# Slot selection by matmul, one small product in float32r and a two-step rounding, in a four-layer gated cross-attention kernel

## The reference

```python
x = x + tanh(g_xattn[n]) * xattn_n(layernorm(x), ctx)      # n = 0..3
x = x + tanh(g_ffn[n])   * ffn_n(layernorm(x))
# xattn_1..3: scores = q_r @ k_r^T (16 heads), softmax over 1500, ctx_c = attn @ kv_rope
# ffn_0, a mixture of 64 experts, 6 of them for each token, at most 64 tokens for each expert:
pos  = cumsum(onehot(expert of each assignment)) - onehot     # place of a token in its expert
keep = pos < 64;  slot = where(keep, pos, 64)
xd = zeros((64, 65, 256)).at[expert, slot].set(x[tok])
yd = relu(xd @ w1^T)**2 @ w2^T
y  = zeros_like(x).at[tok].add(yd[expert, slot] * gate)       # plus a shared expert
# ffn_1, with 8-bit activations and ternary weights:
q(x) = clip(round(x * s), -128, 127) / s,  s = 127 / clip(max|x|, 1e-5)
h = silu(q(x) @ qw_gate^T) * (q(x) @ qw_up^T);  h = rms_norm(h);  out = q(h) @ qw_down^T
```

## Time and profile before

| | |
|---|---|
| median of 3 runs | 2315.12 us (2315.03 to 2316.34) |
| profiled execution, its own time | 2315.12 us |
| its span, first to last instruction | 2313.3 us |
| PE busy | 2175.3 us (94%) |
| DVE, ACT, POOL busy | 1529.8, 1029.6, 1482.9 us |
| mean granted TensorE clock | 0.961 |

### The profile page before, as it was taken

How to read it: one execution, slowest core, us unless ns; L and a number is a source line. 1 busy time by engine, 2 the same in 40 slices (tenths; PEclk the granted TensorE clock), 3 DMA queues, 4 the chain that set the end, 5 groups by cost and what they waited for, 6 DMA issues and landing times.

```text
span 2313.3 us, 31038 instructions
## 1 busy us (share of the span) xinstructions
PE 2175.3 (94%) x11468; PEld 1554.3 (67%) x11468; DVE 1529.8 (66%) x2476; ACT 1029.6 (45%) x1509; POOL 1482.9 (64%) x933
## 2 busy tenths in 40 slices
PE   7788999999999997798999999979998999999988
PEld 5577888766666655565666666668896666666587
DVE  6765662578788755766788888652235788888653
ACT  4452222555555544311454555533434555555443
POOL 0355563288888874366688888824443888888744
PEclk9898999999999998898999999999998999999989
DMA  3114767211111103101111111024531111111022
GB/s 91 48 58 155 239 209 207 70 41 42 59 41 41 47 24 117 39 1 41 41 41 41 57 44 41 8 67 146 145 99 54 41 41 61 40 41 42 7 69 74
DMA packets 60593, 160.16 MB, mean 69 GB/s; under 512 B 9621, under 2 KB 19621, under 8 KB 60060
## 3 DMA queue, kind: packets, MB, share of 16 engines
q1 hardware_dynamic: 60060, 157.86, 22.3%
q10 hardware_dynamic: 384, 0.33, 0.1%
HBM read 143.18 MB, written 14.98 MB: 68 GB/s over the span
## 4 chain that ended last, share of the span: by engine, by line
PE 82%; DVE 6%; POOL 3%; ACT 3%; DMA 2%; issue 2%; SPq 0%; POOLq 0%; ACTq 0%; DVEq 0%
PE psum L893 20%; PE psum L1379 19%; PE psum L1369 10%; PE psum L1350 10%; PE psum L1371 10%; PE psum L1527 2%; PE psum L1396 2%; PE psum L1490 1%; DMA V<-in_ctx 1%; PE psum L1264 1%; POOL CL L1814 1%; PE psum L1550 1%; PE psum L1142 1%; DMA WqrT<-in_a_WrT 1%; DMA bd<-in_blockdiag 1%
## 5 line engine op out<-in xcount | busy, mean ns | idle before, releaser
L1792 ACT ACTIVATE E<-psum 125x896 f32<-125x896 f32 x576 | 528.2, 920 | 576.2 <-PE psum L1371 549.3
L2341 DVE TENSOR_REDUCE mx<-psum 128x1 f32<-128x500 f32 x945 | 611.9, 675 | 165.8 <-PE psum L1350 163.8
L2082 POOL TENSOR_TENSOR SA<-SA,E 125x896 f32<-125x896 f32 x282 | 597.3, 2118 | 22.1
L1379 PE MATMUL psum<-E,V 125*64 125x448 f32 x2304 | 472.0, 544 | 0.0
L1369 PE MATMUL psum<-Q,K 128*125 128x448 f32 x1152 | 331.7, 369 | 2.3 <-ACT E L1792 2.3
L1350 PE MATMUL psum<-K,Q 128*128 128x500 f32 x945 | 329.0, 402 | 2.6 <-ACT Q L1779 2.2
L1371 PE MATMUL psum<-Q,K 128*125 128x448 f32 x1152 | 329.8, 367 | 0.0
L1379 PEld LDWEIGHTS psum<-E,V 125*64 125x64 f32 x2304 | 171.6, 136 | 214.0 <-issue 202.6
L2082 POOL TENSOR_TENSOR SA<-SA,SB 125x896 f32<-125x896 f32 x93 | 194.0, 2086 | 148.7 <-DVE SB L2364 148.7
L1350 PEld LDWEIGHTS psum<-K,Q 128*128 128x128 f32 x945 | 174.4, 188 | 134.2 <-issue 34.6
L1369 PEld LDWEIGHTS psum<-Q,K 128*125 128x125 f32 x1152 | 213.1, 187 | 37.2 <-ACT E L1792 6.9
(11 more groups left out here) (296 smaller groups left out, 3649.0 us busy)
## 6 DMA issues: line engine op xcount, KB each, us to landing
K<-kt_scratch SPq DMA_DIRECT2D x48, 750.0 KB, 5.0
K<-kt_scratch SPq DMA_DIRECT2D x48, 375.0 KB, 6.2
EW<-in_f_w SPq DMA_DIRECT2D x64, 256.0 KB, 4.7
kt_scratch<-kt SPq DMA_DIRECT2D x16, 750.0 KB, 4.7
WS<-in_f_w SPq DMA_DIRECT2D x31, 384.0 KB, 4.8
GB<-gates_scratch SPq DMA_DIRECT2D x36, 224.0 KB, 3.7
slot_of_t<-slots_scratch SPq DMA_DIRECT2D x64, 112.0 KB, 3.3
WoT<-in_a_WoT SPq DMA_DIRECT2D x24, 256.0 KB, 4.2
```

Of the source, the lines that this page charges most:

```text
L1379: i = e.matmul(psum[c * DC:(c + 1) * DC, 4 + b % 2, 0:HT], V[0:LP, b, k * DC:(k + 1) * DC], E[g[n, b, k] % NE][0:LP, half[c]], start=k == ...
L1792: e.activation(E[m % NE][0:LP, :].rearrange("p (c q) -> p c q", c=2), psum[0:LP, pair:pair + 2, 0:HT], ACT.Exp).then_inc(exp_set.sem, 1)
L2082: e.tensor_tensor(SA[b % 2][0:LP, :], a[0:LP, :], x[0:LP, :], ALU.add).then_inc(sum_set.sem, 1)
L2341: e.tensor_reduce(mx[:, b % 2, j * 3 + c:j * 3 + c + 1], psum[:, bank, 0:CW], AX.X, ALU.max).then_inc(small_free.sem, 1)
```

## The change

It has three parts.

1. In the experts of layer 0, `pick` moves from POOL and DMA to PE and ACT. The slot number s (-32 to 32) of each token and expert and its square are transposed together (128 rows: s squared for 64 experts, s for 64 experts) and stay in SBUF as GT, float32r. DVE builds weights for each group in a new task `rows` (L2608 ff., 128 x 512, float32r). For each pair and each half of the tokens, PE multiplies 128 x 128 of these weights with 448 columns of GT, which gives s^2 - 2*s*j for slot j; ACT writes S = relu(1 - j^2 - that) = relu(1 - (s - j)^2), which is 1 on equality and 0 otherwise, into the half of S. The 64 new results of PE take their places in the ring of four PSUM banks; comb waits for S by halves. The scratch in HBM, its write and wait, and the 64 broadcasting DMAs go. The tile slot_of holds two planes, and DVE makes the square (448 elements a partition).
2. In the core attentions, nm and the identity of L1357 become float32r; DVE makes the float32r identity once for each layer, after the memset of nm.
3. In the 8-bit part, `quantise` gets a second DVE instruction, which subtracts the rounding constant and takes the minimum with 127, behind a wait for the first; ACT then only copies.

```diff
-    order += [("st", 1, a) for a in range(4)] + [("pload", q) for q in range(3)]
+    order += [("st", 1, a) for a in range(4)]        # ("rows", 0) now stands behind ("route", 7)
...
-        pick = lambda q: [("pick", q)] + ([("pload", q + 3)] if q + 3 < E0 // 2 else [])
-        steps = [[("ups", g)] + ([("gsl", 0)] if g == 0 else []), pick(q),
+        steps = [[("ups", g)] + ([("gsl", 0)] if g == 0 else []), [("pick", q, 0), ("pick", q, 1)],
                  [("comb", q - 1)] if g > 0 else [], ([("disp", g + 1, 0)] if more else []) + st(0),
-                 [("downs", q), ("downs", q + 1)], pick(q + 1) + st(1), [("comb", q)],
+                 [("downs", q), ("downs", q + 1)], [("pick", q + 1, 0), ("pick", q + 1, 1)] + st(1), [("comb", q)],
                  ([("disp", g + 1, 1)] if more else []) + st(2), [("downs", q + 2), ("downs", q + 3)],
-                 pick(q + 2), [("comb", q + 1)] + st(3),
-                 [("gsl", g + 1)] if more else [], pick(q + 3), [("comb", q + 2)]]
+                 [("pick", q + 2, 0), ("pick", q + 2, 1)] + ([("rows", g + 1)] if more else []), [("comb", q + 1)] + st(3),
+                 [("gsl", g + 1)] if more else [], [("pick", q + 3, 0), ("pick", q + 3, 1)], [("comb", q + 2)]]
...
-        if t[0] in ("disp", "gsl", "ups", "downs"):            # upper_uses
+        if t[0] in ("disp", "gsl", "ups", "downs", "pick"):
...
-                e.matmul(psum[0:DC, bank, 0:P], nm[:, b % 2, :], ident[:, :], start=True, stop=True).then_inc(small_made.sem, 1)
+                e.matmul(psum[0:DC, bank, 0:P], nm[:, b % 2, :], identr[:, :], start=True, stop=True).then_inc(small_made.sem, 1)
...
+            elif kind == "pick":                                # PE
+                q, c = t
+                bank = upper(e, f, kind, q, c)
+                if q == 0:
+                    e.wait_ge(*gt_set.at(f, 1))
+                e.wait_ge(*rows_set.at(q // 4))
+                pair = m["rows"][q // 4 % 2][:, q % 4 * 2:q % 4 * 2 + 2, :].rearrange("p k c -> p (k c)")
+                e.matmul(psum[:, bank, 0:HT], pair, m["GT"][:, half[c]], start=True, stop=True).then_inc(matched.sem, 1)
             elif kind == "comb":
                 q, = t
                 e.wait_ge(*ydl_set.at(q))
-                e.wait_ge(*s_set.at(q))
                 for c in range(2):
+                    e.wait_ge(*s_set.at(q, c))
...
+            elif kind == "pick":                                # ACT
+                q, c = t
+                e.wait_ge(*matched.at(q, c))
+                if q >= 2:
+                    e.wait_ge(*combined.at(q - 2, c))
+                e.activation(m["S"][q % 2][:, half[c]], psum[:, upper_bank[f, (kind, q, c)], 0:HT], ACT.Relu, scale=-1.0,
+                             bias=m["slots"][:, 2 * CAP0 + 16:2 * CAP0 + 17]).then_inc(s_set.sem, 1)
...
-            elif kind == "pick":                                # POOL
-                q, = t
-                e.wait_ge(*pb_in.at(q))
-                if q >= 2:
-                    e.wait_ge(*combined.at(q - 2, 1))
-                e.tensor_scalar(m["S"][q % 2][:, :], m["PB"][q % 3][:, :], m["slots"][:, CAP0:CAP0 + 1], None,
-                                ALU.is_equal).then_inc(s_set.sem, 1)
...
-        e.memset(nm[:, :, :], 0.0).then_inc(*dve_own.up())
+        e.memset(nm[:, :, :].bitcast(F32), 0.0)
+        e.tensor_copy(identr[:, :], ident[:, :]).then_inc(*dve_own.up())
...
-        e.tensor_scalar(x, x, scale, ROUND, ALU.mult, ALU.add).then_inc(signal.sem, 1)
+        e.tensor_scalar(x, x, scale, ROUND, ALU.mult, ALU.add).then_inc(*dve_own.up())
+        e.wait_ge(*dve_own.now())
+        e.tensor_scalar(x, x, ROUND, 127.0, ALU.subtract, ALU.min).then_inc(signal.sem, 1)
...
-                             ACT.Copy, bias=-ROUND).then_inc(xqt_set.sem, 1)
+                             ACT.Copy).then_inc(xqt_set.sem, 1)
```

More of the change, by code:

```diff
@@ L129, in constants @@
     slot = np.tile((np.arange(CAP0) - CAP0 // 2).astype(f), (P, 1))
-    c["slots"] = np.concatenate([slot, slot.T[np.arange(P) % CAP0, 0:1]], 1).astype(f)
+    parts = [slot, np.where(np.arange(P)[:, None] < E0, f(1.0), -2.0 * slot), np.tile(np.arange(8, dtype=f), (P, 1)),
+             (np.arange(P)[:, None] % E0 - 8 * np.arange(NG)[None, :]).astype(f), 1.0 - slot.T[np.arange(P) % CAP0, 0:1] ** 2]
+    c["slots"] = np.concatenate(parts, 1).astype(f)
     return c
@@ L232, in sparse_order @@
     order += [("wload", e) for e in range(4, 12)] + side.pop(0)
-    order += [("route", 6)] + [("st", 0, a) for a in range(4)] + [("route", 7), ("disp", 0, 0), ("route", 8), ("disp", 0, 1)]
-    order += [("st", 1, a) for a in range(4)] + [("pload", q) for q in range(3)]
+    order += [("route", 6)] + [("st", 0, a) for a in range(4)] + [("route", 7), ("rows", 0), ("disp", 0, 0), ("route", 8), ("disp", 0, 1)]
+    order += [("st", 1, a) for a in range(4)]
     for g in range(NG):
@@ L389, in upper_uses @@
             out.append(("pos",))
-        elif t[0] in ("disp", "gsl", "ups", "downs"):
+        elif t[0] in ("disp", "gsl", "ups", "downs", "pick"):
             out.append(t)
@@ L496, in build @@
     mx = mem.take("mx", [P, 2, NT * 3], F32)
-    nm = mem.take("nm", [P, 2, DC], F32)
+    nm = mem.take("nm", [P, 2, DC], F32R)
+    identr = mem.take("ident_r", [P, P], F32R)
     at(norm_at)
@@ L581, in build @@
     m["YtH"] = mem.take("YtH", [P, NT, D], F32R)
-    m["pos"] = mem.take("slot_of", [P, NT, E0], F32)
+    m["pos"] = mem.take("slot_of", [P, NT, 2, E0], F32)
     m["W4"] = mem.take("w_pairs", [P, NT, E0 // 2, 4], F32R)
@@ L587, in build @@
     emask = mem.take("expert_mask", [P, NT, E0], F32)
-    m["PB"] = [mem.take("slot_of_t", [P, T], BF16) for _ in range(2)]
+    m["GT"] = mem.take("slot_of_t", [P, T], F32R)
     m["gs"] = [mem.take("slot_gate", [P, 4], F32) for _ in range(2)]
@@ L619, in build @@
     m["GW"], m["GH"], m["GL"] = (mem.take("gate_" + n, [P, KD, E0], d) for n, d in (("w", F32), ("hi", F32R), ("lo", F32R)))
-    m["slots"] = mem.take("slots", [P, CAP0 + 1], F32)
+    m["slots"] = mem.take("slots", [P, CAP0 * 2 + 17], F32)
     at(w_at)
@@ L639, in build @@
     assert mem.at <= st_end
[L640 to L644, removed]
+    at(norm_at - 2 * 4 * 512)
+    m["rows"] = [mem.take("slot_rows", [P, 8, CAP0], F32R) for _ in range(2)]
     at(yh_at)
@@ L784, in build @@
     groups, by_part = [(g,) for g in range(NG)], [(g, a) for g in range(NG) for a in range(4)]
+    rows_set = flag("slot_rows_set", groups)
     tokens_high, tokens_low = flag("tokens_high", [(i,) for i in tiles]), flag("tokens_low", [(i,) for i in tiles])
@@ L845, in build @@
     wraw_in = Landed(nc, "wraw", 3, [(k, (k,)) for k in range(3)])
-    pb_in = Landed(nc, "", 3, [(q % 3, (q,)) for q in range(E0 // 2)], 2, after=wraw_in)
-    wq_in = Landed(nc, "", 3, [(k, (k,)) for k in range(3)], after=pb_in)
+    wq_in = Landed(nc, "", 3, [(k, (k,)) for k in range(3)], after=wraw_in)
     heads_in = Landed(nc, "heads", 4, [(g, (g,)) for g in range(4)], 2)
@@ L866, in upper_free @@
             return yl_set.at({0: 2, 1: 4, 2: 6}[f], *key)
-        if kind in ("disp", "gsl", "ups", "downs"):
-            return {"disp": xd_set, "gsl": gs_set, "ups": h2_set, "downs": ydl_set}[kind].at(*key)
+        if kind in ("disp", "gsl", "ups", "downs", "pick"):
+            return {"disp": xd_set, "gsl": gs_set, "ups": h2_set, "downs": ydl_set, "pick": s_set}[kind].at(*key)
         return {"pos": pos_free, "fu": u_set, "fm": ml_set, "fg": g_set, "fa": al_set, "cturn": kl_set, "in": xqt_set,
@@ L2520, in dve_route0 @@
             e.wait_ge(*pos_free.at())
-            e.tensor_scalar(rank, rank, 128.0 - CAP0 // 2, CAP0 / 2, ALU.add, ALU.min).then_inc(slot_of_set.sem, 1)
+            e.tensor_scalar(rank, rank, 128.0 - CAP0 // 2, CAP0 / 2, ALU.add, ALU.min).then_inc(*dve_own.up())
+            e.wait_ge(*dve_own.now())
+            e.tensor_tensor(m["pos"][:, :, 0, :], rank, rank, ALU.mult).then_inc(slot_of_set.sem, 1)
         elif step == 7:
```

37 lines of the change are left out of this document (16 added, 21 removed).

## The result

The changed kernel takes 2348.86 us (median of 4 runs, 2344.44 to 2351.06) where the kernel before takes 2315.73 beside it (4 runs, 2315.03 to 2324.15). The ratio is 1.0133, with a 95% interval of 1.0105 to 1.0160: slower by 31 us by the ratio (24 to 37) and by 33 between the medians, where +14.9 was forecast, with an upper end of +27. So the sign was right, and the forecast was about half of what was measured. The profiled execution of the changed kernel spans 2345.6 us.

A forecast was written before the change was run, and what follows sets the result against it. PE was taken to bound the experts and core attention, DVE the 8-bit part. Selection +4.9, rounding +5.3 and spread +4.4 gave +14.6 on 2315.1: 2329.7, given as 2330.0 (chance 0.59), range 2317 to 2342.

The forecast's parts named there:

- first comb earlier: Experts of layer 0: with no pick on POOL, ctx_rot starts earlier and the first comb starts at 192.3, for -5.2 us.
- products and ring: Experts of layer 0: 60 added PE products at 0.20 us, +12.1; small waits from sharing the PSUM banks, +1.5.
- the clock term: Experts of layer 0: shorter first wait and full columns behind four-column bursts return part of the half-clock loss, -3.5 us.
- 12.8 for all lost clock: Experts of layer 0: 2.6 us lost after the first wait plus 10.2 behind six four-column bursts; the most that could return.
- The small waits: Experts of layer 0: PE's waits besides the first comb's, 2.7 us over 16 halves; taken as 0.1 more each, +1.5.
- rival C: Experts of layer 0: the ring of PSUM banks binds, 0.7 us more in each half group, +11.2, 2339.4 us; chance 0.14.
- The 0.6 that the first sequences were to gain: Core attentions: three spreads, first sequence of each layer, stand outside the run of products and gain 0.2 us each.
- Rival A: Core attentions: the float32r spread stays in the run, costing 0.06 instead of 0.22, -7.7 us, 2317.6; chance 0.12.
- the second starts when that has ended, so 0.75: 8-bit part: the second rounding instruction on h follows POOL's multiplication unblocked; 0.76 with its wait, tiles 1 to 6, 4.6 us.
- 7.9 us for a tile: 8-bit part: period of a tile before the change, set by DVE, read from rounding starts of tiles 4 and 6.
- rival D: 8-bit part: the second rounding costs nothing (2324.4), or POOL blocks it in four tiles too, 12.3 us (2336.7); chance 0.07.
- the signs that the text named: Next profile: experts about 5 us longer, picks 0.20 apart, spread to next product 0.3 or more, tile period 8.6 to 8.7.

The follow-up runs named there:

- the last experiment: The kernel before with POOL's second rotation of V ahead of the first pick and the three-operand rounding together; ratio 1.0007 (0.9993 to 1.0021).

## Why the prediction was too low

**Part 1: 4.9 forecast, 10.7 by the stages, 6.0 (2.8 to 9.3) by the medians.** From the first disp to the first spread of layer 1, eight profiles without this part (and with the picks in their old place) take 285.5 to 293.5 us, 288.2 in the mean; three with it in its own order 298.8, 298.9 and 299.0. Taken apart, each half clock counted half:

| term | forecast | measured |
|---|---|---|
| first comb earlier | -5.2 | 25.5 to 20.7: -4.8 |
| first to last comb, products and ring | 12.1 + 1.5 = +13.6 | 195.2 to 210.0: +14.9 |
| last comb to first spread | 0 | 49.4 to 48.8: -0.6 |
| clock | -3.5 | half clock 36.2 to 38.7 us: +1.2 |
| sum | +4.9 | +10.7 |

The products and the ring together and the first comb were sized well, each for partly wrong reasons (below). *The step that failed is the clock term*, -3.5: "part comes back". Full columns behind the bursts did not keep the clock up: it still falls to half behind five of the seven bursts in the stage of the changed kernel (six in its second profile), where it fell behind six. From first to last comb there are 20.5, 23.9 and 23.9 us at half clock, against 18.7 to 35.2, 26.7 in the mean, in the eight profiles without the part. Ahead of the first comb it is 13.7 in one profile and 6.8 in two, against 8.3 to 9.2, of which a part (4.9 of 8.4 in the first profile) fell into PE's wait and cost nothing. (If the lengths up to the first comb are taken as they are, 29.9 and 25.3 in the mean, that term is -4.6 and the clock +1.0; the sum is the same.) And behind the last comb it is 6.8 in all four profiles with this part, against none to 3.4 in the eight. So what the stage gained came back behind it. In three of the four that stretch at half clock begins behind the same short wait that was there before, with the same products ahead of it; before and changed:

```profile
418.12 1.10 PE L1162 MATMUL psum<-G,Wq 128*128 128x64 f32 x8 [0.56 <-DVE ML L2226]
427.85 1.48 PE L1148 MATMUL psum<-G,Wq 128*128 128x64 f32 x8 [0.56 <-DVE ML L2220]
```

I had looked only at the episodes there are, and not at where the next would fall. (The text's own 12.8 for all lost clock was too small as well: the 29.2 us at half clock from first to last comb cost 14.6.) That the part moves the episodes is seen; why they come where they do is not shown by any run here, and stays open. So does the distance between the two measures of this part: other executions of that kernel than the profiled one were shorter, and they have no trace.

The small waits came as rival C had them, though not its size: the 60 products after the first comb cost 20.9 to 22.0 us instead of 12.1, and their neighbours, which wait less, gave back some 7. That the sum of the two is near the forecast's 13.6 is luck. The first comb came as early as forecast, but not with some 3 us of its wait left: PE waited 0.1 us or less in one profile and 0.6 in the two others, since the products of the pick and the half clock filled the time.

**Part 2: +4.4 forecast, +6.1 by the stages, 6.0 by the medians.** The mechanism was right. A spread costs 0.10 out of the run, 0.20 itself and 0.05 into the run, 0.35 instead of 0.22, where 0.12 + 0.12 + 0.09 = 0.33 was forecast; the product itself was sized too low and the two changes too high. The range went to 0.40. The 0.6 that the first sequences were to gain didn't come (1.49 against 1.48), which is a third of what this term lacks. The Trainium skill's rule ("PSUM — Partial Sum Buffer", section "The four PSUM rules") by which float32r forces the full column group is borne out so far as times can show it: a float32r product with 64 columns makes the same 0.10 us step as a float32 one with 128. The same step agrees with the Trainium skill's "TensorEngine Tiling (Array Packing)", section "Key Properties", by which a change of the tiling mode drains the engine; that the 0.10 us are a drain is not shown. Rival A is refuted.

**Part 3: +5.3 forecast, +10.1 by the stages (279.5 in the mean of three profiles with it, 269.4 in that of five without it and without part 1), +13 by its own median.** With part 1 alone, in either order, that stretch takes 271.4 and 271.0, and the changed kernel 7.8 more than these; so part 3 is 8 to 11, and some 2 us lie between the parts. *The step that failed*: "the second starts when that has ended, so 0.75". It holds in the tiles in which the first instruction is blocked, and I applied it to all. In the others the first takes 0.75, and the second starts just as POOL does or 0.3 us behind it. The first instruction is blocked in three tiles before; with the part it is in three or four, partly others, and the second in one or two more, so that four or five of seven tiles are held up instead of three. Without the multiplication the term is 4.9, close to the 5.3. The text's 7.9 us for a tile was that of held-up tiles, too: the others took 6.3 and 6.8. My bound for this, rival D's 12.3, was in the text and given a share of 0.07 with the other end; that was too little. The trace of before had the sign: of the four tiles whose first instruction got through, POOL's multiplication began during it in two (0.25 us behind 913.38 and 0.58 behind 943.32), so a second instruction right behind the first would meet it there, five tiles in all. The two multiplications of before:

```profile
913.63 2.73 POOL L2166 TENSOR_TENSOR h<-h,ln_w 128x1024 f32<-128x1024 f32 x1 [1.94 <-ACT sg L1987]
943.90 2.38 POOL L2166 TENSOR_TENSOR h<-h,ln_w 128x1024 f32<-128x1024 f32 x1 [1.68 <-ACT sg L1987]
```

**The sum.** 10.7 + 6.1 + 10.1 = +26.9 by the stages, +25.5 (21 to 29) by the run of the changed kernel on the second chip, +31 by the ratio (24 to 37) on the first. The forecast of +14.6 lacks 4.7 on the clock, 4.8 on POOL's block, 1.7 on the spread, and 1.3 on the ring, less 0.2 in smaller items. The range was too narrow as well: I gave the bounds above one at a time, and the upper end of +27 holds no two of them together. Of the signs that the text named, some came out: the stage of the experts is longer, the clock behind most bursts is still 0.50, and PE does wait for banks. Others did not: the distance from the spread to the next product is 0.20, not 0.3 or more (the other 0.15 lie in the pairs around it), the picks are 0.35 to 0.37 apart, not 0.20, and the period of a tile is 8.5 to 9.0 instead of 8.6 to 8.7.

## What to carry to other kernels

Before an instruction is added to an engine, see whether the one that is there is slow in some tiles and fast in others while another engine works on the same tile: an added instruction is exposed to the same block in the tiles that used to escape it. A cheaper type is no gain for a small product in a run of half-width products if it makes it full-width: the two changes of width cost 0.15 us here and the product 0.20, against 0.22 in all before. And a gain on the clock should not be booked from the episodes of one trace: here half-clock time left one stretch and came back in the next.

## What was not expected of the hardware

The time at half clock differs widely between executions with nearly the same work on PE: from the first to the last comb it is 18.7 us in the profile of the spread alone, 29.2 in that of before and 55.8 in that of the last experiment. A product of 448 columns behind short ones takes 0.29 us to the next start instead of 0.20: in the changed kernel one starts at 257.11, the weight load (0.19) of the product behind it only at 257.20, and that product at 257.40, as the load ends. And the three-operand form on DVE is no way around POOL: it was held up for 2.90 us as the two-operand form was (2.94 in the run of the third part alone).
